# Six weight transfers in front of a modulation block: other buffers and another order on one queue

## What is computed

```python
mod = (silu(c) @ wmod).reshape(4, 6, 1, 512)
sa, ca, ga, sb, cb, gb = (mod[:, i] for i in range(6))
ga, gb = sign(.) * max(abs(.), 0.25)          # both gates
h = layernorm(x) * (1 + ca) + sa
x = x + ga * attn(h)       # layernorm; Q, K, V; rotary K, V; A = 0.5 * sum_s cos(K) * cos(V) + 0.5
                           # (A * Q) @ W_out + b_out + h
h = layernorm(x) * (1 + cb) + sb
x = x + gb * ffn(h)        # relu(h W_up) W_down + (sum of top-2 softmax) * h W_expert
```

## Time and profile before

| | |
|---|---|
| median of 3 runs | 373.13 us |
| range of these runs | 371.59 to 373.65 us |
| the profiled execution, its own time | 374.51 us |
| span of its instructions | 372.4 us |
| mean granted TensorE clock | 0.991 |
| TensorE matmul busy | 352.7 us, 95% of the span |
| VectorE, ScalarE, GpSimd busy | 245.3, 165.9, 123.2 us |
| transfers | 27.45 MB, mean 74 GB/s |

### The profile page before, as it was taken

The page is one execution under the profiler, slowest core; times in us unless marked ns, Lnnn a source line. Parts: engine busy times, 40 slices in busy tenths (PEclk is TensorE's granted clock), DMA queues, the critical chain, the costliest instruction groups (busy, mean ns, idle before and its releaser), DMA issues.

```text
span 372.4 us, 4910 instructions
## 1 busy us (share of the span) xinstructions
PE 352.7 (95%) x1776; PEld 286.6 (77%) x1776; DVE 245.3 (66%) x501; ACT 165.9 (45%) x317; POOL 123.2 (33%) x128
## 2 busy tenths in 40 slices
PE   3969699999999999999999999999999999999996
PEld 1327377788887888888888888988988898889885
DVE  1788969758978588785887458427812772282374
ACT  1466858684437811376115692237043514441110
POOL 0086664994931529315262051920000010000000
PEclk9989899999999999999999999999999999999999
DMA  6988665540020000000000003100200020011003
GB/s 198 386 328 282 257 226 159 192 160 2 1 84 0 2 0 19 12 1 0 2 28 2 0 0 114 29 2 28 87 0 0 35 80 2 0 58 57 0 2 114
DMA packets 10968, 27.45 MB, mean 74 GB/s; under 512 B 1200, under 2 KB 1584, under 8 KB 9792
## 3 DMA queue, kind: packets, MB, share of 16 engines
q1 hardware_dynamic: 10944, 27.13, 20.7%
HBM read 22.90 MB, written 4.23 MB: 73 GB/s over the span
## 4 chain that ended last, share of the span: by engine, by line
PE 71%; DVE 9%; issue 7%; DMA 5%; ACT 4%; POOL 3%; SPq 1%; POOLq 0%; DVEq 0%; ACTq 0%
PE ps L1177 22%; PE ps L1179 22%; PE ps L1178 22%; DMA stage<-in_wmod 3%; PE ps L1225 3%; DMA xs<-in_X 2%; PE ps L1202 1%; DVE hst L781 1%; ACT z L587 1%; POOL w_lo L386 1%; POOL hrs L383 1%; DVE hb L771 1%; ACT ps L599 1%; ACT t_hi L601 1%; POOL xrs L354 1%
## 5 line engine op out<-in xcount | busy, mean ns | idle before, releaser
L1177 PE MATMUL ps<-wv_hi,t_hi 128*128 128x260 f32 (+1 forms) x192 | 61.7, 321 | 1.0 <-issue 0.6
L1179 PE MATMUL ps<-wv_hi,t_lo 128*128 128x260 f32 (+1 forms) x192 | 61.4, 320 | 0.0
L1178 PE MATMUL ps<-wv_lo,t_hi 128*128 128x260 f32 (+1 forms) x192 | 61.3, 319 | 0.0
L1177 PE MATMUL ps<-t_hi,w_hi 128*128 128x512 f32 x128 | 50.7, 396 | 0.8 <-DVE sb_col L1045 0.8
L1177 PE MATMUL ps<-w_hi,g_hi 128*128 128x512 f32 (+1 forms) x132 | 51.3, 389 | 0.0
L1179 PE MATMUL ps<-w_hi,g_lo 128*128 128x512 f32 (+1 forms) x132 | 50.6, 384 | 0.0
L1178 PE MATMUL ps<-w_lo,g_hi 128*128 128x512 f32 (+1 forms) x132 | 50.6, 383 | 0.0
L1179 PE MATMUL ps<-t_hi,w_lo 128*128 128x512 f32 x128 | 50.0, 391 | 0.0
L1178 PE MATMUL ps<-t_lo,w_hi 128*128 128x512 f32 x128 | 49.9, 390 | 0.0
L1177 PEld LDWEIGHTS ps<-wv_hi,t_hi 128*128 128x128 f32 x192 | 36.0, 188 | 4.7 <-issue 1.7
L1179 PEld LDWEIGHTS ps<-wv_hi,t_lo 128*128 128x128 f32 x192 | 36.1, 188 | 2.9
(11 more groups left out here) (151 smaller groups left out, 718.6 us busy)
## 6 DMA issues: line engine op xcount, KB each, us to landing
stage<-in_w SPq DMA_DIRECT2D x4, 1024.0 KB, 6.1
out<-xs SPq DMA_DIRECT2D x15, 256.0 KB, 2.0
xs<-in_X SPq DMA_DIRECT2D x3, 1024.0 KB, 9.1
xs<-in_wmod SPq DMA_DIRECT2D x8, 256.0 KB, 6.0
stage<-in_w SPq DMA_DIRECT2D x8, 256.0 KB, 8.1
stage<-in_wmod SPq DMA_DIRECT2D x2, 1024.0 KB, 9.7
gate_bc<-mod_rows SPq DMA_DIRECT2D x8, 256.0 KB, 3.4
xs<-in_X SPq DMA_DIRECT2D x2, 512.0 KB, 7.0
```

The lines of the kernel that those rows point to most:

```text
L1177: mm(dst, l_hi, r_hi, start=start, stop=False)
L1178: mm(dst, l_hi, r_lo, start=False, stop=False)
L1179: return mm(dst, l_lo, r_hi, start=False, stop=stop)
```

## The change

Four buffers and three places in SP's order are changed. No instruction of TensorE, VectorE, ScalarE or GpSimd is added, removed or moved; only addresses of their operands change. On SP no transfer is added or removed. The helper `load_component(i)` holds the same one transfer as L306, L310, L314 and L316.

```diff
-        mod_raw, mod_abs, mod_sign, gate_rows = (stage[:, 1, i * D:(i + 1) * D] for i in range(4))
+        mod_raw, mod_abs, mod_sign, gate_rows = (xs[:, (3 * NT + i) * D:(3 * NT + i + 1) * D] for i in range(4))

-        MODS = ((2, x_slot(2)), (5, gate_bc[:]), (4, stage[:, 0, :]), (3, stage[:, 1, :]))
+        MODS = ((2, x_slot(2)), (5, gate_bc[:]), (4, x_slot(3)), (3, stage[:, 0, :]))

-        w_raw = (stage[:, 0, :], stage[:, 1, :], x_slot(3), stage[:, 0, :], stage[:, 1, :], stage[:, 0, :], stage[:, 1, :])
+        w_raw = (stage[:, 0, :], stage[:, 1, :], stage[:, 1, :], stage[:, 0, :], stage[:, 1, :], stage[:, 0, :], stage[:, 1, :])

-            sp.dma_start(MODS[1][1], wmod[MODS[1][0]]).then_inc(wm_in[MODS[1][0]], 16)
+            def load_component(i):
+                comp, weights = MODS[i]
+                sp.dma_start(weights, wmod[comp]).then_inc(wm_in[comp], 16)
+
+            load_component(1)
             sp.wait_ge(mod_sb, 1)
             sp.dma_start(mod_rows[ROW_CA], rows[0:B, :]).then_inc(row_out, 16)
             sp.dma_start(mod_rows[ROW_SA], rows[32:32 + B, :]).then_inc(row_out, 16)
-            sp.dma_start(MODS[0][1], wmod[MODS[0][0]]).then_inc(wm_in[MODS[0][0]], 16)
             sp.wait_ge(row_out, 32)
             load_modulation(1)
+            load_component(0)
+            load_component(2)
             sp.wait_ge(wlo_k, NC)
-            sp.dma_start(MODS[2][1], wmod[MODS[2][0]]).then_inc(wm_in[MODS[2][0]], 16)
+            load_component(3)
             sp.wait_ge(wlo_v, NC)
-            sp.dma_start(MODS[3][1], wmod[MODS[3][0]]).then_inc(wm_in[MODS[3][0]], 16)
             sp.dma_start(w_raw[2], w[2]).then_inc(w_in[2], 16)
@@
+            sp.wait_ge(modt_ps, 1)
+            load_x(3)
             sp.wait_ge(wlo_q, NC)
-            load_x(3)
-            sp.wait_ge(modt_ps, 1)
             sp.dma_start(w_raw[4], w[4]).then_inc(w_in[4], 16)
```

## The result

| | before | changed |
|---|---|---|
| median | 373.28 us (13 runs) | 376.09 us (13 runs) |
| range | 370.97 to 374.13 | 374.67 to 376.63 |
| profiled execution, its own time | 374.51 | 374.94 |
| its span, mean granted clock | 372.4, 0.991 | 372.9, 0.986 |

The ratio is 1.0072 with a 95% interval of [1.0052, 1.0092], some 2.7 us. Forecast were 373.9 us, a range of 372.0 to 375.9 and "same" at 0.78; slower by over 0.5% had 0.15. The median lies above the range.

What follows compares the result with a forecast made beforehand. TensorE, waiting ahead of `mod_rest` for component 3's transfer, was taken as the bound. Component 2's later place (+1.0) and the clock (-0.2) summed to +0.8 us on 373.13, giving 373.9 us, range 372.0 to 375.9.

Steps and rivals of the forecast that it cites:

- What bounds the kernel: Ahead of `mod_rest`: TensorE waits 3.0 us for component 3's transfer, and its delay passes on almost one for one.
- Components 4 and 3, Q's weights, gates, batch 3 of x, all at 0: SP's queue and buffers: earlier issue, later Q weights and new addresses were each claimed to be worth 0.
- Component 2 behind the spread rows, +1.0: SP's queue: the transfers before component 3's landing start 1.12 us later, costing +1.0 us, bounds +0.5 to +1.4.
- Clock, -0.2: In `mod_rest`: the low stretch covers less or equal work after the later start, gain 0.4 or 0, middle -0.2 us.
- Rival B: In `mod_rest`: the clock stays low for a second stretch, +1.7 with +1.0, 375.8 us; chance 0.12.
- Rivals A (with D): Transfers ahead of `mod_rest`: ramp or engine backlog swallows the delay, or nothing changes; middle 373.1 us; chance 0.22.
- C: Spread rows at the queue's head cost only their bytes; TensorE waits 0.5, clock stays up, 368.9 us; chance 0.05.
- The sentence on one profile: Clock term's remark: slow matmuls differ in number from run to run, which one profile can't show; no size given.

Runs made afterwards that it cites:

- buffers_only: Changed kernel with the order of issue of the kernel before, so only the buffers differ: 1.0014 of the kernel before.
- one_back: Changed kernel with only component 2 moved back ahead of the wait for the row stores: 0.9988 of the kernel before.
- the filled kernels: Useless matmuls added ahead of `mod_rest`, 9 in the kernel before and 16 in the changed kernel: 0.9961 and 0.9998 of the kernel before.
- order_only: Kernel before with one line moved, component 2 issued behind the two spread rows, buffers as before: 1.0078 of the kernel before.
- one_early: Kernel before with component 4 issued early, component 3 and Q's weights right behind the spread rows, own buffers for components: 371.64 us, 0.9945.
- after_again: The changed kernel without an edit, run once more for a second trace: 1.0070 of the kernel before.
- early_act: Kernel before with components 4 and 3 early, row stores issued from ScalarE, component 2 and Q's weights right behind the spread rows: 1.0009.

## Why the prediction was wrong, step by step

- **What bounds the kernel: right.** TensorE waits for component 3, the delay goes through almost one for one (+1.4 in landing and +1.4 in time after the first store, between traces with the low clock in both), nothing later takes it up: the wait for `sb_col` is 0.8 in both, and batch 2 of x is again issued right behind the end of `mod_rest`, at 48.33.
- **Components 4 and 3, Q's weights, gates, batch 3 of x, all at 0: right.** The ratios of `buffers_only` and `one_back` are within 0.002 of 1, with intervals from 0.996 to 1.004. ScalarE's L640 came at 48.34, forecast 48.6.
- **Component 2 behind the spread rows, +1.0: right in kind, too small.** It was issued at 29.42, behind the wait as described. The landing is +1.6 over nine traces, above my upper end of 1.4, and +1.4 in time between the filled kernels. The 1.12 of later issue was counted; not counted was that the spread rows at the head leave engines idle (share 0.35 in `order_only`, 0.66 in the changed kernel) while in mid-stream the share was 0.83. That the idle engines are what costs the other 0.5 us is my reading of these shares; no run separates it. I had a row for it, 0.53 at 105 to 108 us, and read from it only its GB/s.
- **Clock, -0.2: wrong, also in sign, and the step that took the time out of the range.** It was about +1.2, good to a microsecond. I took the profiled execution's low stretch as a fixed part of the kernel before, and asked only how the change would move it. By the two groups of times it was in about half of its executions. The three times shown, 371.59 beside 373.13 and 373.65, lie 1.5 and more apart, about what the low stretch in `mod_rest` costs (1.7), and I took the spread for scatter. The profiled execution's offset of 1.4 is another matter: the median of 373.13 is itself in the upper group, and about 0.5 to 1.0 of the offset had already arisen before the first store, which was issued at 27.31, in `buffers_only` and `one_back` at 26.78 and 26.34. The changed kernel's longer stall had the low clock behind it in all three traces of that order (stall 4.2 to 4.5), and in all 31 executions as far as the mean clock tells. So the sum was some +1.4 and +1.2, where the forecast had +1.0 and -0.2.
- **Rival B (0.12)** had the right place and mechanism, and the wrong condition: it asked for a second stretch on top of the first. What the traces show is a first one in the executions that had none; a second one is likely in at least five of the 31 executions, by their mean clock, and was traced only in a variant. Its price, 375.8, was near the 376.09 measured, in part by luck: its 1.0 + 1.7 comes near the 1.4 + 1.2 measured.
- **Rivals A (with D) and C: wrong.** The spread rows at the head cost more than in mid-stream, not less or only their bytes. The Trainium skill's formula (DMA: Bandwidth & Descriptors, Anatomy of one DMA), a fit for transfers issued from GpSimd, would give 10.4 us from the first issue of the set to landing, as an estimate. The trace disagrees: the changed kernel, which issues from SP, took 42.92 - 28.55 = 14.4.
- **The sentence on one profile: right, and not used.** The two traces of the kernel before have 5.34 and 3.64 us for the same 32 matmuls. The Trainium skill (TensorE: Matmul & The Clock Gate, Part 1) says that the same kernel meets a different number of slow matmuls from run to run. The traces agree. I had cited it and then not let it touch the sum.

What stays open is why 2 KB rows at the head of an empty queue hold back the transfers issued behind them while engines are free, what decides whether the clock falls after a stall of 2.5 to 3.2 us, and how the changed kernel's upper group (376 us and more) divides.

## What to carry to other kernels

A stall of TensorE costs its length and a chance of running the next matmuls at half clock: here in about half of the executions at 2.5 to 3.2 us, and in all that were traced at 4.2 to 4.5. A microsecond more of stall went with a higher chance, so its price wasn't linear. A gain at one stall can be lost at the next, as in `one_early`. If the few times at hand lie apart by what a low stretch costs, ask whether the low stretch of the profiled execution is in all of them, before anything is summed on it. In this kernel a wait on the issuing queue should have a large transfer ahead of it and not behind it, and its small stores, which something waits for, should have no more bytes in front of them than the waiter can spare: 1 MB was a gain, 2 MB a loss.

## What the runs showed that I had not expected

- A small store issued on ScalarE's queue took as long behind 2 MB of SP's transfers as one on SP's own (5.46 and 5.01 us); behind 1 MB 2.71, in the changed kernel with none ahead 1.41 (`after_again`).
- Nine matmuls of no use in a stall are a gain: 0.9961 [0.9935, 0.9987] for the kernel before. In its trace the next 32 take 3.64 us instead of 5.34.
- The wait of 1.8 us for `sb_col` in `one_early` had 3.4 us at 1.2 GHz behind it, where the wait of 2.6 in `early_act` had none.
